# Two states in one pass in the two narrow groups, norm statistics on ScalarE and the first product on VectorE, in a state-space block with adapter and feed-forward layers

## The reference, cut to what matters

```python
x = x + attn(rotate(x, delta_t))         # attn: the part below, twice (forward, reversed), then reduce, gelu, glu
x = x + ffn(expert_linear(x, expert_id))

# layer norm
mu = x.mean(-1); var = ((x - mu) ** 2).mean(-1)
xn = (x - mu) * rsqrt(var + EPS) * ln_g + ln_b
# selective scan, 256 channels d, 16 states n, over the 128 tokens of a sequence
delta = softplus(dt @ dt_proj_w.T + dt_proj_b)
h[d, n] = exp(delta[d] * A[d, n]) * h[d, n] + delta[d] * u[d] * B[n]
y[d]    = sum_n h[d, n] * C[n] + u[d] * D[d]
y = y * silu(z)
```

## Time and profile before

| | us |
|---|---|
| median of 3 runs (999.14 to 1003.47) | 999.75 |
| the profiled execution, device time | 998.47 |
| its span | 996.6 |
| VectorE busy | 894.6 (90%) |
| TensorE busy | 909.4 (91%) |
| GpSimd busy | 845.6 (85%) |
| ScalarE busy | 796.5 (80%) |
| mean granted TensorE clock | 0.974 of full speed |

### The profile page before, as it was taken

How to read it: one execution, slowest core, us unless ns; L and a number is a source line. 1 busy time by engine, 2 the same in 40 slices (tenths; PEclk the granted TensorE clock), 3 DMA queues, 4 the chain that set the end, 5 groups by cost and what they waited for, 6 DMA issues and landing times.

```text
span 996.6 us, 14200 instructions
## 1 busy us (share of the span) xinstructions
PE 909.4 (91%) x4552; PEld 610.2 (61%) x4552; DVE 894.6 (90%) x688; ACT 796.5 (80%) x1294; POOL 845.6 (85%) x427
## 2 busy tenths in 40 slices
PE   5798677879999999999999999999999988999988
PEld 3455546666755676557755666556755775667557
DVE  2899999999999999999999999999999999998610
ACT  6968876988699977998699977898698868888632
POOL 0689999999899998999999898999999999787400
PEclk9799799999999999999999999999999999999999
DMA  4867564754553846556454755557375475565100
GB/s 116 291 205 225 182 193 163 214 185 139 186 167 110 261 145 201 170 174 223 127 181 127 243 164 168 164 183 235 118 246 155 153 196 165 137 206 140 47 1 17
DMA packets 97817, 167.54 MB, mean 168 GB/s; under 512 B 9936, under 2 KB 33552, under 8 KB 97488
## 3 DMA queue, kind: packets, MB, share of 16 engines
q1 hardware_dynamic: 97744, 166.64, 54.5%
HBM read 159.26 MB, written 7.34 MB: 167 GB/s over the span
## 4 chain that ended last, share of the span: by engine, by line
PE 40%; DVE 21%; issue 14%; ACT 14%; POOL 9%; DMA 1%; DVEq 0%; SPq 0%; POOLq 0%; ACTq 0%
DVE bank_d L1025 14%; PE bank_y L1315 9%; PE bank_m L1232 7%; POOL state L637 7%; PE bank_m L1148 6%; PE bank_m L1225 4%; ACT bank_d L796 4%; DVE state L1023 3%; ACT L668 3%; DVE state L1030 2%; PE bank_m L1243 2%; PE bank_m L1174 2%; PE bank_m L1198 2%; POOL state L642 2%; PE bank_m L1207 2%
## 5 line engine op out<-in xcount | busy, mean ns | idle before, releaser
L637 POOL TENSOR_TENSOR state<-du,b_rows 128x1024 f32<-128x1024 f32 (+1 forms) x288 | 622.3, 2189 | 47.3 <-PE bank_y L1315 41.5
L1025 DVE TENSOR_TENSOR_SCAN bank_d<-bank_d,state 128x1024 f32<-128x1024 f32 (+1 forms) x225 | 460.9, 2048 | 10.4 <-ACT bank_d L796 9.4
L796 ACT ACTIVATE bank_d<-delta,a_neg 128x512 f32<-128x512 f32 (+1 forms) x540 | 322.9, 634 | 67.6 <-DVE state L1030 62.2
L1315 PEld LDWEIGHTS bank_y<-ident,state 128*128 128x128 f32 x2048 | 243.6, 145 | 75.1 <-issue 66.0
L1315 PE MATMUL bank_y<-ident,state 128*128 128x128 f32 x2048 | 265.4, 281 | 15.0 <-DVE gated L1041 14.2
L1030 DVE TENSOR_TENSOR state<-bank_d,c_rows 128x1024 f32<-128x1024 f32 (+1 forms) x225 | 248.4, 1104 | 6.7
L642 POOL TENSOR_TENSOR state<-state,c_rows 128x1024 f32<-128x1024 f32 (+1 forms) x63 | 133.8, 2124 | 11.5 <-DVE state L1023 11.4
L1148 PE MATMUL bank_m<-xnT,w_conv 128*128 128x508 f32 (+7 forms) x288 | 117.0, 552 | 2.9 <-DVE x1T L1050 2.2
L1232 PE MATMUL bank_m<-hidA,h_s 128*128 128x512 f32 (+1 forms) x256 | 108.1, 568 | 4.6 <-ACT hidA L868 4.3
L1225 PE MATMUL bank_m<-hidB,h_s 128*128 128x512 f32 (+1 forms) x256 | 107.4, 567 | 0.3 <-DVE hidB L1064 0.2
L1023 DVE TENSOR_TENSOR_SCAN state<-bank_d,state 128x1024 f32<-128x1024 f32 (+1 forms) x45 | 91.9, 2042 | 1.0 <-ACT bank_d L796 1.0
(11 more groups left out here) (148 smaller groups left out, 1040.3 us busy)
## 6 DMA issues: line engine op xcount, KB each, us to landing
b_rows<-bc_store SPq DMA_DIRECT2D x256, 256.0 KB, 5.1
c_rows<-bc_store SPq DMA_DIRECT2D x256, 256.0 KB, 4.8
wsel<-merged SPq DMA_DIRECT2D x32, 512.0 KB, 3.4
merged<-hidA SPq DMA_DIRECT2D x8, 512.0 KB, 3.1
h_s<-in_h SPq DMA_DIRECT2D x2, 1024.0 KB, 8.8
xin<-in_x SPq DMA_DIRECT2D x7, 256.0 KB, 5.4
out<-cT SPq DMA_DIRECT2D x7, 256.0 KB, 3.0
wsel<-in_factors SPq DMA_DIRECT2D x8, 160.0 KB, 3.6
```

The costliest lines, as they stand in the source:

```text
L637: nc.gpsimd.tensor_tensor(split(unit_state(u)), du[:, d, :, :width(g)], per_half(b_rows, u), ALU.mult).then_inc(S.bx_ready, 1)
L796: ins = act.activation(split(unit_decay(u))[:, h], delta[:, d, h, :width(g)], ACT.Exp, scale=a_neg[:, h, n:n + 1])
L1025: dve.tensor_tensor_scan(decay, decay, drive, 0.0, ALU.mult, ALU.add).then_inc(S.scanned, 1)
L1315: ins = pe.matmul(bank_y[:, h, s * P:(s + 1) * P], split(unit_state(u))[:, h, s * LEN:(s + 1) * LEN], ident[:, :], start=(n == 0 and s == ...
```

## The change

In the narrow groups two states of one direction make one pass: `drive`, `scan` and `weigh` are each one instruction of 1024 columns where there were two of 512. The exponentials and the sums on TensorE stay as many as before (four activations and eight transposing products for a pass). `passes` lists the units at which a pass begins, `through(u)` counts passes, and rings, rooms and semaphores count passes. GpSimd weighs four passes of a narrow group, which are eight units (`POOL_PASSES`), where it weighed seven units. The passes in the room `early` are those of units 8 and 18 (`AHEAD_PASSES`), and neither is among GpSimd's any more: VectorE scans and weighs them there.

For groups 1 to 8 ScalarE makes the norm statistics, four `Copy` activations with a summed output and four `Square` activations with bias and summed output (two and two in group 8), at two new places of `ACT_AT`. Group 0's stay on VectorE, ahead of its timeline. VectorE makes the first product of the kernel (pass 0) and marks the starts for it. `a_neg` is made later, the table of exponentials is loaded ahead of group 0's `dbc0`, and a wait on `y_turned` in `take_u` becomes one on `skipped`. All tables of numbers are drawn up anew; the timeline begins at -80 where it began at -48.

```diff
+POOL_UNITS, POOL_PASSES = (3, 8, 12, 17, 21, 26, 30), (4, 12, 20, 28)
+AHEAD, AHEAD_PASSES, AHEAD_LEAD = (8, 17), (8, 18), 5
...
-ACT_AT = {"scale": (-43.5, -41.5, -41.5, -36.5, -36.5, -41, -41),
+ACT_AT = {"scale": (-76.5, -78.5, -40, -37, -36.5, -47, -48),
...
+          "stats": (-78.5, -55.5, -36.5, -33.5, -32.5, -42.5, -39.5),
+          "aggr": (-72, -34.5, -35.5, -29.5, -29, -41.5, -39)}
...
-FIRST, STEP, END = -48.0, 0.5, 96.0
+FIRST, STEP, END = -80.0, 0.5, 96.0
...
+        def states_in(u):
+            return 2 if PAIRS[u // UNITS] < max(PAIRS) else 1
+        passes = [u for u in range(TOTAL) if u % states_in(u) == 0]
+        serial = {u: i for i, u in enumerate(passes)}
...
+        def input_of(u):
+            g, d, n = unit(u)
+            w, k = width(g), states_in(u)
+            if k > 1:
+                return du[:, d, :, :w].unsqueeze(1).to_broadcast([P, k, HALVES, w])
+            return du[:, d, :, :w]
...
             def drive(u):
                 g, d, n = unit(u)
+                if u == 0:
+                    return
...
-                wait(pool, S.states_summed, u + 1 - RING)
-                nc.gpsimd.tensor_tensor(split(unit_state(u)), du[:, d, :, :width(g)], per_half(b_rows, u), ALU.mult).then_inc(S.bx_ready, 1)
+                wait(pool, S.states_summed, through(u) - RING)
+                nc.gpsimd.tensor_tensor(split(unit_state(u), u), input_of(u), per_half(b_rows, u), ALU.mult).then_inc(S.bx_ready, 1)
...
+            def norm_sums(g):
+                act.wait_ge(S.cond_done, g + 1)
+                for t in range(sequences(g)):
+                    ins = act.activation(scaled[:, t // 2, t % 2], xc[:, t // 2, t % 2], ACT.Copy, accum_out=moments[:, t, 0:1])
+                ins.then_inc(S.summed, 1)
+                act.wait_ge(S.summed, g)
+                act.activation(neg_mean[:, :sequences(g)], moments[:, :sequences(g), 0], ACT.Copy, scale=-1.0 / HID).then_inc(S.mean_ready, 1)
+
+            def norm_squares(g):
+                act.wait_ge(S.mean_ready, g)
+                for t in range(sequences(g)):
+                    ins = act.activation(scaled[:, t // 2, t % 2], xc[:, t // 2, t % 2], ACT.Square, bias=neg_mean[:, t:t + 1],
+                                         accum_out=moments[:, t, 1:2])
+                ins.then_inc(S.squares_summed, 1)
...
-                for h in range(HALVES):
-                    ins = act.activation(split(unit_decay(u))[:, h], delta[:, d, h, :width(g)], ACT.Exp, scale=a_neg[:, h, n:n + 1])
+                for k in range(states_in(u)):
+                    for h in range(HALVES):
+                        ins = act.activation(block_of(unit_decay(u), u, k, h), delta[:, d, h, :width(g)], ACT.Exp,
+                                             scale=a_neg[:, h, n + k:n + k + 1])
...
+                if g == 0 and name == "dbc0":
+                    return EXP_LN
...
+                dve.wait_ge(S.du_ready, 1)
+                dve.memset(delta[:, 0, :, :w].rearrange("p h (b t) -> p h b t", t=LEN)[:, :, :, 0:1], FORGET).then_inc(S.starts_marked, 1)
+                wait_row(dve, b_loaded, 0)
+                dve.tensor_tensor(split(unit_state(0), 0), input_of(0), per_half(b_rows, 0), ALU.mult).then_inc(S.bx_ready, 1)
```

219 lines of the change are left out of this document (118 added, 101 removed), and 136 rows, old and new, of tables (FILL, TAKE_LAG, VEC).

## The result

| | before | after |
|---|---|---|
| median, the two run side by side | 999.44 us (998.53 to 1003.47) | 1010.15 us (1009.76 to 1011.94) |
| ratio, 95% interval | | 1.0102 (1.0079 to 1.0126) |
| first scan starts | 30.43 | 31.37 |
| group 0, from its first scan to group 1's | 68.9 | 70.7 |
| the seven wide groups together | 774.4 | 783.5 |

What follows compares the result with a forecast made beforehand. VectorE was taken as the bound from the first scan until just before 940 us, with a tail behind. Terms -7.9 - 8.2 + 1.5 + 1.0 - 1.1 + 1.5 = -13.2 us took 998.5 to 985 us (forecast 978 to 990; 8 in 10: 974 to 996).

Steps and rivals of the forecast that it cites:

- the term of -7.9: Norm statistics of groups 1 to 8 leaving VectorE's list save 7.9 us, 1.17 us in each of six wide groups.
- The rival of an engine that holds the wide groups: TensorE or GpSimd paces the wide groups, so the statistics' gain returns as waits: 993 us (989 to 995), chance 0.16.
- The pairs: Two states in one pass save VectorE 4.1 us in each of the two narrow groups, -8.2 us.
- pairs without effect: Rival: products and scans over two states cost as much as two of 512 columns; 992 to 998 us, chance 0.09.
- `early`*, +1.0 with an end at 7: Narrow groups' decays kept in SBUF: four more VectorE weighings from there at 0.25 us each, +1.0 us, between 0 and 7.
- More work on ScalarE: Statistics add about 3 us per wide group on ScalarE, mostly fitting its idle time: +1.5 us, between 0 and +21.
- The slower rival: In wide groups, statistics between a gelu's table loads and the next decays make VectorE wait: 1004.5 us, chance 0.09.
- The start: First scan comes 1.5 to 2 us later, at 31.9 to 32.5 us, through ScalarE's added work: +1.5 us.
- Deeper rooms in group 8: Rooms of 1024 columns take back half of VectorE's 2.3 us of waits for decays there: -1.1 us, between 0 and -2.3.
- The rest at 0: Number of DMAs and products unchanged, one reordering in the tail: 0, within 1 us either way.
- ScalarE too late: Sign of a wrong forecast: VectorE's waits for decays above 25 us would show ScalarE's statistics delaying them.
- not by 20 to 25: Sign of a right forecast: ScalarE's busy time up by 20 to 25 us, its wait for rooms down by about as much.

Runs made afterwards that it cites:

- e10: Kernel before with only the first product and mark of the starts moved to VectorE; no pairs, statistics on VectorE, old numbers: 1000.52 us, ratio 1.0016.
- e9: Kernel before with first product by VectorE and pairs in group 8 alone; statistics on VectorE, old numbers: 1001.77 us, ratio 1.0024.
- e3: Changed kernel with statistics back on VectorE and all old numbers, so pairs and first product alone: 1008.81 us, ratio 1.0096.
- e1: Changed kernel with the norm statistics of groups 1 to 8 back on VectorE; pairs, first product and new numbers stay: 1009.87 us, ratio 1.0107.
- e2: Changed kernel with all tables of numbers of the kernel before, statistics still on ScalarE: 1032.04 us, ratio 1.0316.
- e4: Kernel before with only the statistics of groups 1 to 8 moved to ScalarE, no pairs, old numbers: 1029.11 us, ratio 1.0287.
- e6: Changed kernel without the statistics of groups 1 to 8 on any engine (constants in the norm): 1005.88 us, ratio 1.0054.
- e5: Kernel before without the statistics of groups 1 to 8 on any engine (constants in the norm): 999.54 us, ratio 0.9999.
- e12: Kernel before with statistics on ScalarE, plus a second room for xc so those of groups 3 to 8 stand 14 to 18 numbers earlier: 1020.41 us, ratio 1.0216.
- e15: Changed kernel with the sums and squares of group 7 alone put back at their old numbers (-34 and -34): 1012.66 us, ratio 1.0148.
- e13: Changed kernel with GpSimd's step sizes of group 0's reversed direction at 9.5 instead of 8, inputs at 11.5 instead of 10: 1006.43 us, ratio 1.0082.
- e7: Changed kernel with GpSimd weighing passes (8, 12, 18, 28) instead of (4, 12, 20, 28): 1017.26 us, ratio 1.0163.
- e8: Changed kernel with the decays of pairs ordered 3 numbers ahead of their scan instead of 2: 1023.30 us, ratio 1.0217.
- e11: Changed kernel with no pass of the narrow groups in `early`: 1021.38 us, ratio 1.0212.
- e14: e3 with GpSimd's step sizes of group 0's reversed direction at 9.5 instead of 6.5, inputs at 11.5 instead of 10.5: 1011.55 us, ratio 1.0126.

## Why the prediction was wrong, point by point

One path of single steps from the kernel before to the changed one, by the ratios:

| step | ratio | from | share |
|---|---|---|---|
| first product by VectorE | 1.0016 | e10 | +1.6 us |
| pairs in group 8 | 1.0024 | e9 | +0.8 |
| pairs in group 0 | 1.0096 | e3 | +7.2 |
| new numbers, statistics on VectorE | 1.0107 | e1 | +1.1 |
| statistics to ScalarE | 1.0102 | the change | -0.5 |

The shares are 1000 us times the difference of two ratios; only the third is clearly beyond the intervals. Another path gives other shares: with old numbers the last step costs 23 to 30 us (e2 over e3, e4 over before). The parts don't add. Small shares also hide gains and losses at different places. The same kernels by stage, one profiled execution each, in us:

| | first scan | group 0 | group 1 | groups 2 to 7 | from group 8 |
|---|---|---|---|---|---|
| before | 30.4 | 68.9 | 108.8 | 665.6 | 122.9 |
| e9, pairs in group 8 | 29.8 | 69.4 | 108.8 | 666.2 | 123.0 |
| e3, pairs in both | 29.3 | 77.0 | 113.0 | 663.7 | 123.1 |
| e1, and new numbers | 30.5 | 71.5 | 112.9 | 668.1 | 122.6 |
| the change | 31.4 | 70.7 | 114.1 | 669.4 | 122.3 |
| e6, the change without statistics | 30.1 | 68.9 | 115.2 | 668.3 | 123.0 |
| e5, before without statistics | 31.0 | 69.0 | 108.8 | 663.1 | 122.9 |

The changed kernel's 11.3 us of span lie at the start (0.9), in group 0 (1.9), in group 1 (5.3) and in groups 2 to 7 (3.8), and -0.6 behind them. Group 1's 5.3 us are its two scans from `early` (8.6 us against 5.6) and its waits for decays (3.4 against 0.3). The new numbers take 5.5 us off group 0 and add 4.4 to groups 2 to 7 (e1 over e3); they add 5.2 there where no engine makes statistics (e6 over e5), with 3.5 us of waits for TensorE that e5 lacks and scans from `early` 1.6 us longer. Which number does it is open.

- *"What the change takes off VectorE's list after the first scan counts in full as long as the other three ... keep up"* is the step that failed, and with it the term of -7.9. The size was right (e5: 8.0 us less work), the worth was 0, within 2 us. The 10 us of named waits of VectorE were read as slack of the others. But an engine that hardly waits doesn't show that the next one is far behind. With 8 us off VectorE's list, its waits for ScalarE's decays and GpSimd's products grew by about as much. The statistics stand just ahead of the borders, where ScalarE sets the time even in the kernel before (the rows in e5). The rival of an engine that holds the wide groups had 0.16; it named TensorE and GpSimd, and in e5 the waits were mostly for ScalarE.
- *The pairs*, -8.2: wrong. The start-to-start prices hold in the trace. In group 8 the last scan did start sooner (61.3 us behind the first against 63.8), but what follows took back 1.9 of that, 1.1 of it by the last scan's own length, so that the whole from its first scan is 0.6 shorter. In group 0, GpSimd, ScalarE and TensorE also have the expert weights and the first front to make. That work in larger pieces means longer stays behind a blocked instruction there fits the waits, but no run shows it by itself. With old numbers the pairs cost 7.6 us in group 0 and 4.2 in group 1 (e3 over e9); with the new ones group 0 is 70.7, and group 1 stays long. The rival "pairs without effect" allowed 0, not a loss.
- *`early`*, +1.0 with an end at 7: too small. The four weighings cost 1942 ns each against 1223, 2.9 us: nearly three times the 1.0, and 0.6 of the 5 that I had worked out from the rule of the Trainium skill (SBUF — State Buffer, "Who interferes with whom") and set aside. The four scans cost 2916 against 2286, 2.5 us, of which 0.7 were paid before the change too. Besides, the wide groups' scans lost 5.3, which the sum had nowhere. The rows at 130.19 and 71.24 show single collisions; no run kept the leads and took the collisions away.
- *More work on ScalarE*, +1.5 with an end at 21: the work was sized rightly (3.2 us a group in e4), and the price was 4.3 in the changed kernel (e6) and 29.6 with old numbers (e4 over e5). "ScalarE idles 62.2 us for rooms alone, so most of it fits" was the weak sentence. Those 62 us are a sum over the span. In the kernel before, ScalarE's idle time in a wide group lies mostly between numbers 8 and 20 (the rows in e12), and the statistics stand around the border, from 27 to 3. The slower rival (0.09) named a mechanism, its place and 1004.5 us. e4 and e15 show it at a border, 4.65 and 4.66 us. The changed kernel doesn't show it: its waits of 1.57 us stand at the borders of e5 and e6 as well, and what the statistics cost it lies at the start and in group 0, as far as two profiled executions tell.
- *The start*, +1.5: right (31.37 us, so +0.9; in e13 and e15, with the same front, 32.5 and 32.6). *Deeper rooms in group 8*, -1.1: the scans gained, the end didn't. *The rest at 0*: the new numbers are worth nothing in all to the kernel with statistics on VectorE (e1 over e3) and over 20 us to the one with them on ScalarE (the change over e2).

Of the signs named, VectorE's waits for decays (22.2 us in all) stayed below the 25 that would have told "ScalarE too late", and ScalarE's wait for rooms fell by 7 us, not by 20 to 25. The forecast had 0.08 for slower. Three of its terms rested on one premise, VectorE as the only bound, and were given as if they could fail one by one.

Open: which link carries the pairs' loss in group 0. Changes of one link each (e7, e8, e11, e13, e14) left group 0 the same or made it longer. Also open: how much of groups 1 to 7 the longer scans from `early` cost by themselves, and whether GpSimd's later rows of B play a part. Its waits for them rose from 5.7 to 17.4 us in the wide groups, though VectorE never waits there for a product. TensorE's granted clock in group 0 was 0.88 before, 0.79 after and 0.82 in e3. The table of stretches, 90 to 100 us, before and after:

```profile
90.00:100.00 10.00, 7.44 (x39) 4.32 (x37) 9.80 (x17) 8.07 (x18) 8.85 (x6) 1.00 0.79 261
```
```profile
90.00:100.00 10.00, 8.64 (x38) 6.10 (x36) 10.00 (x9) 9.87 (x32) 9.73 (x6) 0.72 0.75 239
```

At the lower clock TensorE is busy 8.6 us of the ten with about as many instructions as took 7.4 before; no run tells how much of the loss that is.

## What to carry to other kernels

Where four in-order engines are each busy 80 to 91%, take the work off the supposed bound in an experiment (e5) before pricing its move: 8 us off VectorE were worth 0. Price work, added or taken off, at the place in the list where it stands and by the slack there, not by the engine's idle time as a whole. Larger instructions can cost where other work waits behind them: during a crowded start they made a group of 69 us one of 77 (e9 and e3). Before a step of a path is called free, compare the stages: a total that stood still hid 5.5 us gained and 4.4 lost (e3 and e1).
